# A four-layer graph network on one core: how the edge lists, their neighbours and the first weights are fetched

## The chip, the cores and the metric

The kernel runs on 1 core of one Trainium2 chip. The metric is the device time of one execution in microseconds (us). Before the change it is 2734.12 us, the median of 3 runs (2732.61 to 2734.6).

## The reference, cut to what matters

There are 3125 nodes with 256 features (`x`) and 53125 edges, sorted by destination. Four layers follow one another; each normalises `x`, computes something per edge, reduces it per destination node and adds it to `x`.

```python
src, dst = src[argsort(dst)], dst[argsort(dst)]       # edges sorted by destination
h = maximum(layernorm(x), 0)
# layer 0: message passing with a sum
msg = relu(concat([h[src], h[dst]]) @ W_msg + b_msg)
agg = segment_sum(msg, dst)
u   = relu(concat([h, agg]) @ W_upd + b_upd)
x   = x + (u - mean(u)) * rsqrt(var(u) + 1e-5) * gamma + beta
# layer 1: sum, mean and max of edge attributes, and an MLP
# layer 2: attention over the edges (segment max, exp, segment sums)
# layer 3: maximum over weighted neighbours
g = relu(maximum(layernorm(x), 0) @ W_pool.T + b_pool)
neigh = segment_max(g[src] * edge_weight, dst)
x   = x + h @ W_self.T + b_self + neigh @ W_neigh.T + b_neigh
```

Because the edges are sorted by destination, a node's edges stand in a row. Whether an edge is the first or the last of its node is seen by comparing its destination with that of the edge before it and of the edge after it. This is why the kernel needs the neighbours of every edge, across the borders of its own tiling too.

## The kernel before, in words

The kernel is a row of stages, each a `nc.Block()` with one instruction stream per engine; a stage begins when all engines have ended the one before. The change touches three of them.

**The opening** (`opening`, from L252). It does three things at once.

- It loads `x` in five parts of five blocks of 125 nodes (SyncE's queue, L325), normalises it, and computes two tables: h times the upper half of W_msg (the source table) and h times the lower half plus bias (the window table). For each of the 25 blocks: ScalarE makes `h` (L376), TensorE turns it (L400), VectorE copies the turned block to `hT` (L476), TensorE multiplies (L411), ScalarE copies the source half out of PSUM (L381), VectorE adds the bias to the window half (L458), and SyncE (L333) and GpSimd (L357) store the two to HBM. `scales(c)` computes mean and scale of part c on VectorE; its one step on ScalarE is the square root (L373). `scales(0)` comes first; `scales(1)` stands in front of the `hT` copy of block 0, `scales(2)` in front of that of block 5, and so on.
- It reads the edge lists in rows of 128 edges, 104 rows x 4 on the partitions (`src_rows`, `dst_rows`), and makes from them the lines that mark first and last edges, with 17 dependent VectorE steps ("links", L491 to L513). Between one link and the next, VectorE does one block of the work above (`next_block`). The neighbour of each row's first edge is in a tile of its own, `before`, that of its last edge in `after`; each is filled by five DMAs. All these loads, and the two of `base` (first node of each row), are issued on ScalarE's queue (L365) ahead of everything else ScalarE does: 18 DMAs. VectorE waits for all 18 (`dve.wait_ge(loads, loaded)`) after `scales(0)` and before its first link.
- It does the same for the edges split in 128 lanes of 416 (`lane_dst`, `lane_last`, 3 more DMAs on ScalarE's queue, L368), with 16 further links (`lane_flags`, L545 to L564).

SyncE's order in the opening: the five loads of `x`, then a wait for the 17 links, then the three lines to HBM (L330), and only then the 25 stores of the source table, each behind a wait for its block. TensorE turns the edge rows after block 18 (`edges_at = lines_made + 1`).

**The message pass** (`sum_pass`, from L676) follows. GpSimd gathers 416 tiles of 128 rows of the source table by indirect DMA (L735), each with indices that SyncE fetches (L628). In this pass SyncE first loads the four weight tensors of the update stage (`self.load(sp, *ahead)`, L672), then the first indices.

**The last maximum** (`lane_max_pass`): a running maximum over each lane on VectorE. Three small VectorE memsets set its starting values to 0.

```python
transfers += [(before[:, q:q + 1], ends[q * RT - 2:(q + 1) * RT - 2, :]) for q in range(1, RQ - 1)]
...
act.wait_ge(clears, 4)
for tile, flat in transfers:
    act.dma_start(tile, flat, allow_slow_non_contiguous=True).then_inc(loads, 16)
```

Of the kernel before, what the change touches and what calls it, by code (L numbers as in the profile page):

```python
# [28 lines left out]
I32 = mybir.dt.int32  # L29
ALU = mybir.AluOpType  # L30
# [3 lines left out]
P = 1 << P_BITS  # L34
N = 3125
E = 53125
# [14 lines left out]
RQ = 4  # L51
RT = T // RQ
FULL = E // P
REST = E - FULL * P
# [10 lines left out]
FLT = 3.3895313892515355e38  # L65
# [5 lines left out]
LANE = -(-E // P)  # L71
LANES_FULL = E // LANE
# [36 lines left out]
class Kernel:  # L109
# [140 lines left out]
    def opening(self):  # L250
# [20 lines left out]
        lines_made, lane_steps = 17, 16  # L271
        edges_at = lines_made + 1
        with ExitStack() as ctx:
            def tmp(name, shape, dt=F32):
                return self.sb(name, shape, dt, ctx)
            raw = {k: tmp(k, [RT, RQ, P], I32) for k in ("src_rows", "dst_rows")}
            before, after = tmp("before", [RT, RQ], I32), tmp("after", [RT, RQ], I32)
            src_f, dst_f, other = (tmp(k, [RT, RQ, P]) for k in ("src_f", "dst_f", "other"))
            before_f, after_f = tmp("before_f", [RT, RQ]), tmp("after_f", [RT, RQ])
# [3 lines left out]
            lane_dst, lane_last = tmp("lane_dst", [P, LANE], I32), tmp("lane_last", [P, 1], I32)  # L283
            lane = {k: tmp(f"lane_{k}", [P, LANE]) for k in ("dst_f", "flag", "when")}
            lane.update({k: tmp(f"lane_{k}", [P, 1]) for k in ("last_f", "cut", "whole", "row", "own", "spare")})
# [11 lines left out]
            transfers = []  # L297
            for tile, flat in ((raw["dst_rows"], a["dst"]), (raw["src_rows"], a["src"])):
                transfers += [
                    (tile[:, 0:RQ - 1, :], flat[0:whole * P].rearrange("(q r c) -> r q c", r=RT, c=P)),  # L300
                    (tile[0:FULL - whole, RQ - 1, :], flat[whole * P:FULL * P].rearrange("(r c) -> r c", c=P)),
                    (tile[FULL - whole:FULL - whole + 1, RQ - 1, 0:REST],
                     flat[FULL * P:E].rearrange("(r c) -> r c", r=1))]
            dst = a["dst"]
            ends = dst[P:FULL * P].rearrange("(j c) -> j c", c=P)[:, P - 1:P]
            firsts = dst[P:FULL * P].rearrange("(j c) -> j c", c=P)[:, 0:1]
            transfers += [(before[1:2, 0:1], dst[P - 1:P].rearrange("(r c) -> r c", r=1)),
                          (before[2:RT, 0:1], ends[0:RT - 2, :])]
            transfers += [(before[:, q:q + 1], ends[q * RT - 2:(q + 1) * RT - 2, :]) for q in range(1, RQ - 1)]
            transfers += [(before[0:FULL + 1 - whole, RQ - 1:RQ], ends[whole - 2:FULL - 1, :])]  # L310
            transfers += [(after[:, q:q + 1], firsts[q * RT:(q + 1) * RT, :]) for q in range(RQ - 1)]
            transfers += [(after[0:FULL - 1 - whole, RQ - 1:RQ], firsts[whole:FULL - 1, :]),
                          (after[FULL - 1 - whole:FULL - whole, RQ - 1:RQ],
                           dst[FULL * P:FULL * P + 1].rearrange("(r c) -> r c", r=1))]
            transfers += [(self.base[0:1, 0:FULL], dst[0:FULL * P].rearrange("(j c) -> c j", c=P)[0:1, :]),
                          (self.base[0:1, FULL:FULL + 1], dst[FULL * P:FULL * P + 1].rearrange("(r c) -> r c", r=1))]
            lane_transfers = self.by_lanes(lane_dst, dst) + [
                (lane_last[1:P, :], dst[0:LANES_FULL * LANE].rearrange("(p t) -> p t", t=LANE)[:, LANE - 1:LANE])]
            loaded, lane_loaded = 16 * len(transfers), 16 * len(lane_transfers)

            with nc.Block() as block:
                @block.sync
                def _(sp):
                    for c, of in enumerate(parts):
                        sp.dma_start(self.x[:, of.start:of.stop, :], a["x"][of.start * NT:of.stop * NT, :].rearrange(  # L325
                            "(b p) d -> p b d", p=NT)).then_inc(x_in[c], 16)
                    sp.wait_ge(chain, lines_made)
                    lines = ((self.mask_line, mask), (self.place_line, rel16), (self.carry_line, carry))
                    for line, rows in lines:
                        sp.dma_start(line.rearrange("(q r c) -> r q c", r=RT, c=P), rows[:]).then_inc(lines_out, 16)  # L330
                    for b in range(NB):
                        sp.wait_ge(copied, b + 1)
                        sp.dma_start(self.source_table[b * NT:(b + 1) * NT, :], by_source[:, b, :]  # L333
                                     ).then_inc(sources_out, 16)
                    sp.wait_ge(lines_out, 16 * len(lines))
                    sp.wait_ge(sources_out, 16 * NB)

                @block.gpsimd
                def _(pool):
# [88 lines left out]
                def _(dve):  # L428
                    nc.vector.memset(lane_dst[:], N).then_inc(lane_clears, 1)
                    nc.vector.memset(lane_last[:], -1).then_inc(lane_clears, 1)  # L430
                    nc.vector.memset(raw["dst_rows"][:], -1).then_inc(clears, 1)
                    nc.vector.memset(raw["src_rows"][:], 0).then_inc(clears, 1)
                    nc.vector.memset(before[:], -1).then_inc(clears, 1)
                    nc.vector.memset(after[:], -1).then_inc(clears, 1)
# [56 lines left out]
                    link(nc.vector.tensor_copy(src_f[:], raw["src_rows"][:]))  # L491
                    link(nc.vector.tensor_copy(dst_f[:], raw["dst_rows"][:]))
                    link(nc.vector.tensor_copy(before_f[:], before[:]))
                    link(nc.vector.tensor_copy(after_f[:], after[:]))

                    link(nc.vector.tensor_tensor(rel[:], dst_f[:], dst_f[:, :, 0:1].to_broadcast([RT, RQ, P]),
                                                 ALU.subtract))
# [7 lines left out]

                    link(nc.vector.tensor_copy(other[:, :, 1:P], dst_f[:, :, 0:P - 1]))
                    link(nc.vector.tensor_copy(other[:, :, 0:1], before_f[:].unsqueeze(2)))
                    link(nc.vector.tensor_tensor(flag[:], dst_f[:], other[:], ALU.not_equal))
# [6 lines left out]
                    self.lane_flags(dve, lane, lane_loads, lane_loaded, lane_dst, lane_last, lane_marks, when_made,  # L515
# [13 lines left out]
    def lane_flags(self, dve, lane, loads, loaded, dst, last, marks, when_made, lane_steps, fill, placed):  # L529
# [16 lines left out]
        link(nc.vector.tensor_copy(lane["last_f"][:], last[:]))  # L546
        link(nc.vector.tensor_tensor(flag[:, 1:LANE], dst_f[:, 1:LANE], dst_f[:, 0:LANE - 1], ALU.not_equal))
        link(nc.vector.tensor_tensor(flag[:, 0:1], dst_f[:, 0:1], lane["last_f"][:], ALU.not_equal))
# [125 lines left out]
    def sum_pass(self, name, table, width, window_table, window_width, attention, ahead=None):  # L674
# [14 lines left out]
        with ExitStack() as ctx:  # L689
# [14 lines left out]
            with nc.Block() as block:  # L704
                @block.sync
                def _(sp):
# [15 lines left out]
                    if ahead:  # L722
                        self.load(sp, *ahead)
# [88 lines left out]
                def _(act):  # L812
                    if attention:
                        act.wait_ge(zeroed, 1)

# [1225 lines left out]
    def lane_max_pass(self, name, table, w_self, loaded, biases):  # L2041
# [13 lines left out]
        with ExitStack() as ctx:  # L2055
# [20 lines left out]
            with nc.Block() as block:  # L2076
# [99 lines left out]
                def _(dve):  # L2176
                    nc.vector.memset(none[:], 0.0).then_inc(cleared, 1)
                    nc.vector.memset(ends[:, :, 0:1], 0.0).then_inc(cleared, 1)
# [4 lines left out]
                    nc.vector.memset(end[:], 0.0).then_inc(stepped, 1)  # L2183
# [85 lines left out]
```

## Time and profile before

| | us |
|---|---|
| median of 3 runs | 2734.12 |
| profiled execution, its own time | 2734.72 |
| its span | 2732.6 |
| PE busy | 1354.9 |
| DVE busy | 1588.9 |
| POOL busy | 1390.0 |
| ACT busy | 672.6 |

PE is TensorE's matmuls, PEld its weight loads, DVE is VectorE, ACT ScalarE, POOL GpSimd, SP SyncE. A name with q (ACTq, SPq) is the engine's sequencer, where DMAs are issued; the duration of such a row is how long the issue held that queue, not the transfer. In brackets behind a row of the timeline stands how long the engine sat idle before it, and what ended the wait. No engine is busy for more than 58% of the span: the stages have different limits, so the profile has to be read stage by stage. The page's slices show DMA, TensorE and VectorE nearly idle at the very start of the span, and the opening ends at about 126 us.

### The profile page before, as it was taken

To read this page: it belongs to the slowest core of one execution; us is meant where nothing else is said; L and a number is where in the kernel's file an instruction comes from. 1 tells how busy PE (TensorE), PEld (TensorE's weight loads), DVE (VectorE), ACT (ScalarE), POOL (GpSimd) and SP (SyncE) were. 2 spreads that over 40 slices of the span, in tenths; PEclk is the share of its full clock that TensorE was granted. 3 is DMA by queue.
4 is the path that set the end of the run, shared out by engine and by line. 5 is a ranking of instruction groups with operands and counts; after the bars stand their busy time and mean duration, and the time that the engine had idled before them with its cause. 6 is when DMAs were issued, how large, how long until landed. Compare 5 with 4: busy or idle time off the path is not lost. (4 is left out here: it accounts for less than half of the span.)

```text
span 2732.6 us, 26946 instructions
## 1 busy us (share of the span) xinstructions
PE 1354.9 (50%) x7570; PEld 1070.0 (39%) x7570; DVE 1588.9 (58%) x3262; ACT 672.6 (25%) x1528; POOL 1390.0 (51%) x1444
## 2 busy tenths in 40 slices
PE   3577877877669999997993000000002411111104
PEld 2466766776569999554553000000001300000003
DVE  2467777776769999731213776677675334433432
ACT  1112222221547777111111000000002233333331
POOL 2177777776300000301104777777744377777774
PEclk9889999999879999998997555555555655555557
DMA  2477777875065564101002666666642466666664
GB/s 79 118 236 237 233 233 235 238 228 151 1 181 153 154 154 117 42 2 17 13 12 63 201 216 218 201 208 214 211 161 65 139 213 208 209 212 207 211 212 134
DMA packets 272030, 433.06 MB, mean 158 GB/s; under 512 B 108749, under 2 KB 181031, under 8 KB 271883
## 3 DMA queue, kind: packets, MB, share of 16 engines
q1 hardware_dynamic: 202635, 247.61, 27.3%
q0 software_dynamic: 66784, 183.09, 24.9%
q8 instruction: 62, 1.02, 0.2%
q10 hardware_dynamic: 2464, 0.64, 0.1%
q14 instruction: 85, 0.70, 0.1%
HBM read 302.15 MB, written 128.80 MB: 158 GB/s over the span
## 5 line engine op out<-in xcount | busy, mean ns | idle before, releaser
L1757 POOL DMA_INDIRECT att_rows<-att_table,lane_source x416 | 416.4, 1001 | 126.7 <-issue 126.7
L2083 POOL DMA_INDIRECT best_rows<-message_source_table,lane_source x416 | 393.3, 946 | 167.5 <-issue 126.4
L735 POOL DMA_INDIRECT msg_rows<-message_source_table,msg_index x416 | 400.0, 962 | 147.8 <-issue 125.2
L2194 DVE SCALAR_TENSOR_TENSOR best_state<-best_state,lane_line,best_ps_rows 128x256 f32<-128x256 f32 x416 | 199.8, 480 | 316.2 <-ACT best_ps_rows L2108 297.9
L863 PE MATMUL msg_ps_sum<-msg_by_edge,msg_rows 128*128 128x128 f32 x1664 | 232.4, 299 | 109.3 <-DVE aggT L795 107.6
L1789 PE MATMUL att_ps_upto<-ident,att_largest 128*4 128x128 f32 x1 | 0.4, 375 | 564.1 <-DVE att_largest L1854 564.1
L863 PEld LDWEIGHTS msg_ps_sum<-msg_by_edge,msg_rows 128*128 128x128 f32 x1664 | 218.0, 210 | 140.3 <-issue 139.1
L2108 ACT ACTIVATE best_ps_rows<-best_rows,lane_weight 128x256 f32<-128x256 f32 x416 | 173.5, 462 | 359.2 <-DMA best_rows<-message_source_table,lane_source 359.2
L2142 PE MATMUL best_ps_self<-w_selfT,hT 128*125 128x256 f32 x100 | 51.7, 671 | 398.3 <-DVE x L2200 387.2
L847 PE MATMUL msg_ps_window<-msg_window,msg_by_node 128*128 128x256 f32 x832 | 209.0, 397 | 26.5 <-DMA msg_window<-message_window_table 21.4
L1789 PEld LDWEIGHTS att_ps_upto<-ident,att_largest 128*4 128x4 f32 x1 | 0.1, 83 | 564.8 <-DVE att_largest L1854 564.8
L818 ACT ACTIVATE msg_rows<-msg_rows 128x1024 f32<-128x1024 f32 x104 | 109.9, 1057 | 443.8 <-DVE msg_rows L760 443.8
L1089 PE MATMUL attr_ps_placed<-attr_ends,attr_by_edge 128*97 128x128 f32 x1664 | 201.0, 274 | 0.3 <-ACT aggT L998 0.3
L760 DVE TENSOR_TENSOR msg_rows<-msg_ps_window,msg_rows 128x1024 f32<-128x1024 f32 x104 | 126.9, 1220 | 127.4 <-DMA msg_rows<-message_source_table,msg_index 125.9
L1876 DVE SCALAR_TENSOR_TENSOR aggT<-aggT,lane_carry,att_rows 128x260 f32<-128x260 f32 x388 | 190.3, 491 | 13.6
L2142 PEld LDWEIGHTS best_ps_self<-w_selfT,hT 128*125 128x125 f32 x100 | 28.9, 320 | 420.7 <-DVE x L2200 403.8
L1089 PEld LDWEIGHTS attr_ps_placed<-attr_ends,attr_by_edge 128*97 128x97 f32 x1664 | 186.2, 165 | 0.5 <-issue 0.5
L795 DVE TENSOR_TENSOR aggT<-aggT,msg_ps_sum 128x256 f32 x416 | 172.0, 413 | 24.2 <-DVE aggT L795 20.7
L847 PEld LDWEIGHTS msg_ps_window<-msg_window,msg_by_node 128*128 128x128 f32 x832 | 160.3, 203 | 46.7 <-DVE msg_by_node L748 21.6
L1347 POOL MEMSET att_wc<- 128x512 f32 x1 | 0.5, 519 | 337.1 <-POOLq L907 337.1
L1366 POOL DMA_INDIRECT att_terms<-aggT,first_edge x25 | 29.5, 1178 | 275.5 <-ACT aggT L1533 195.1
L998 ACT COPY aggT<-attr_ps_placed 97x256 f32 x416 | 158.3, 380 | 42.1 <-ACT aggT L998 27.9
(290 smaller groups left out, 2711.9 us busy)
## 6 DMA issues: line engine op xcount, KB each, us to landing
att_states<-aggT SPq DMA_DIRECT2D x104, 528.0 KB
msg_window<-message_window_table SPq DMA_DIRECT2D x416, 128.0 KB
best_states<-best_state SPq DMA_DIRECT2D x104, 512.0 KB
attr_rows<-in_edge_attr SPq DMA_DIRECT2D x103, 192.0 KB, 3.3
msg_line<-place_line SPq DMA_DIRECT2D x52, 256.0 KB, 4.9
attr_line<-mask_line SPq DMA_DIRECT2D x52, 256.0 KB, 3.9
attr_carry<-carry_line SPq DMA_DIRECT2D x52, 256.0 KB
msg_rows<-message_source_table,msg_index POOLq DMA_INDIRECT x416
```

Of the source, the lines that this page charges most:

```text
L735: nc.gpsimd.indirect_dma_start(rows[:, s, t, :], None, table, bass.IndirectOffsetOnAxis(ap=index[:, s, t:t + 1], axis=0)).then_inc(self.ro ...
L760: nc.vector.tensor_tensor(rows[:, s, :, :], ps_window[s % 2][:], rows[:, s, :, :], ALU.add).then_inc(ev["added"], 1)
L795: nc.vector.tensor_tensor(at, at, ps_sum[s % 2][:, t, :, :], ALU.add).then_inc(tile_added[t], 1)
L847: last = nc.tensor.matmul(ps_window[s % 2][:, t, :], by_node[:, s % BUFS, t * P:(t + 1) * P], window[:, s % BUFS, t, k * window_width:(k + ...
L863: last = nc.tensor.matmul(ps_sum[s % 2][:, t, k, :], rows[:, s, t, k * P:(k + 1) * P], by_edge[:, s % BUFS, t, :], start=True, stop=True)
L998: nc.scalar.copy(outT[:, :, bass.ds(bases[t], P)], ps_placed[s % 2][:, t, :, :]).then_inc(stored[t], 1)
L1089: last = nc.tensor.matmul(ps_placed[s % 2][:, t, k, :], by_edge[:, s % BUFS, t, k * bw:(k + 1) * bw], ends[:, s % BUFS, t, :], start=True, ...
L1757: nc.gpsimd.indirect_dma_start(rows[:, t % ring, :], None, self.attention_table, bass.IndirectOffsetOnAxis(ap=self.lane_source[:, t:t + 1] ...
L1876: nc.vector.scalar_tensor_tensor(out=state[:, t % held, 0:H * HS], in0=carried[:] if starts else state[:, (t - 1) % held, 0:H * HS], scala ...
L2083: nc.gpsimd.indirect_dma_start(rows[:, g % SLOTS, t, :], None, table, bass.IndirectOffsetOnAxis(ap=self.lane_source[:, g * TG + t:g * TG + ...
L2108: last = nc.scalar.activation(weighed_row(n), rows[:, g % SLOTS, t, :], ACT.Copy, scale=self.lane_weight[:, n:n + 1])
L2194: nc.vector.scalar_tensor_tensor(out=state[:, g % STATE_BUFS, t, :], in0=before, scalar=self.lane_line[:, n:n + 1], in1=weighed_row(n), op ...
```

## The change

- The tiles of destinations get two more columns: a row is fetched together with its left and right neighbour, as one run of 130 numbers that overlaps the next row's run. `before` and `after` and their ten DMAs go, and so do six links. The lanes get one more column in the same way; `lane_last` and two links go. In all there are 11 and 14 links.
- The eight edge-row loads are issued on GpSimd's queue, ahead of the loads of W_msg and its bias. ScalarE's queue keeps only the three lane loads, now split in rows 0, 1 to 126, and 127.
- The two `base` loads go to SyncE's queue, behind `x`.
- SyncE stores the source table's first 12 blocks, then waits for the links and stores the three lines, then goes on with the blocks. TensorE turns the edge rows after block 12.
- GpSimd's clearing of `aggT` is three memsets instead of one.
- In the message pass the update weights are loaded from ScalarE's queue instead of SyncE's.
- In the last maximum the starting values are the lowest number, not 0.

```diff
-        lines_made, lane_steps = 17, 16
+        lines_made, lane_steps = 11, 14
...
+            def run_of(first, rows, size):
+                return bass.AP(dst.tensor, dst.offset + first, [[step, n] for step, n in rows] + [[1, size]])
+            full_rows = FULL - whole
+            transfers = [
+                (dst_rows[0:1, 0, 1:P + 2], run_of(0, [(P, 1)], P + 1)),
+                (dst_rows[1:RT, 0, :], run_of(P - 1, [(P, RT - 1)], P + 2)),
+                (dst_rows[:, 1:RQ - 1, :], run_of(RT * P - 1, [(P, RT), (RT * P, RQ - 2)], P + 2)),
+                (dst_rows[0:full_rows, RQ - 1, :], run_of(whole * P - 1, [(P, full_rows)], P + 2)),
+                (dst_rows[full_rows:full_rows + 1, RQ - 1, 0:REST + 1], run_of(FULL * P - 1, [(P, 1)], REST + 1)),
+                (src_rows[:, 0:RQ - 1, :], src[0:whole * P].rearrange("(q r c) -> r q c", r=RT, c=P)),
+                (src_rows[0:full_rows, RQ - 1, :], src[whole * P:FULL * P].rearrange("(r c) -> r c", c=P)),
+                (src_rows[full_rows:full_rows + 1, RQ - 1, 0:REST], src[FULL * P:E].rearrange("(r c) -> r c", r=1))]
+            lane_transfers = [
+                (lane_dst[0:1, 1:LANE + 1], run_of(0, [(LANE, 1)], LANE)),
+                (lane_dst[1:LANES_FULL, :], run_of(LANE - 1, [(LANE, LANES_FULL - 1)], LANE + 1)),
+                (lane_dst[LANES_FULL:P, 0:LANE_REST + 1],
+                 run_of(LANES_FULL * LANE - 1, [(LANE, 1)], LANE_REST + 1))]
...
 SyncE, opening
-                    sp.wait_ge(chain, lines_made)
+                    for tile, flat in first_nodes:
+                        sp.dma_start(tile, flat, allow_slow_non_contiguous=True).then_inc(lines_out, 16)
-                    for line, rows in lines:
-                        sp.dma_start(line.rearrange("(q r c) -> r q c", r=RT, c=P), rows[:]).then_inc(lines_out, 16)
                     for b in range(NB):
+                        if b == edges_at:
+                            sp.wait_ge(chain, lines_made)
+                            for line, rows in lines:
+                                sp.dma_start(line.rearrange("(q r c) -> r q c", r=RT, c=P), rows[:]
+                                             ).then_inc(lines_out, 16)
                         sp.wait_ge(copied, b + 1)
...
 GpSimd, opening
+                    pool.wait_ge(clears, 2)
+                    for tile, flat in transfers:
+                        pool.dma_start(tile, flat, allow_slow_non_contiguous=True).then_inc(loads, 16)
...
-                    nc.gpsimd.memset(self.aggT[:], 0.0)
+                    for k in range(3):
+                        nc.gpsimd.memset(self.aggT[:, k, :], 0.0)
...
 ScalarE, opening
-                    act.wait_ge(clears, 4)
-                    for tile, flat in transfers:
-                        act.dma_start(tile, flat, allow_slow_non_contiguous=True).then_inc(loads, 16)
...
 VectorE, opening (the neighbours are slices of the same tile)
+                    own = dst_f[:, :, 1:P + 1]
-                    link(nc.vector.tensor_copy(other[:, :, 0:P - 1], dst_f[:, :, 1:P]))
-                    link(nc.vector.tensor_copy(other[:, :, P - 1:P], after_f[:].unsqueeze(2)))
-                    link(nc.vector.tensor_tensor(flag[:], dst_f[:], other[:], ALU.not_equal))
+                    link(nc.vector.tensor_tensor(flag[:], own, dst_f[:, :, 2:P + 2], ALU.not_equal))
...
 message pass
-                    if ahead:
-                        self.load(sp, *ahead)
...
+                    if ahead:
+                        self.load(act, *ahead)
...
 last maximum
-                    nc.vector.memset(ends[:, :, 0:1], 0.0).then_inc(cleared, 1)
+                    nc.vector.memset(ends[:, :, 0:1], -FLT).then_inc(cleared, 1)
...
-                    nc.vector.memset(end[:], 0.0).then_inc(stepped, 1)
+                    nc.vector.memset(end[:], -FLT).then_inc(stepped, 1)
```

## Rows read from the trace of the kernel before

**Rows 1.** One of the page's costliest groups: busy, mean ns | idle before, releaser.

```profile
L735 POOL DMA_INDIRECT msg_rows<-message_source_table,msg_index x416 | 400.0, 962 | 147.8 <-issue 125.2
```

**Rows 2.** GpSimd's waits, whole run: us in total, times, longest.

```profile
POOL msg_rows L735 <- issue: 125.2, 411, 0.3
...
POOL msg_rows L735 <- DMA msg_index<-source: 21.4, 1, 21.4
...
POOL msg_rows L735 <- PE msg_ps_sum L863: 1.2, 4, 0.3
```

**Rows 3.** Timeline of the first 50 us: start, duration, instruction, [idle <- releaser].

```profile
0.76 27.83 SPq L325 DMA_DIRECT2D x<-in_x  x5
...
1.57 1.69 POOL L347 DMA_DIRECT2D msg_w<-in_L_gnn_W_msg  x2
...
2.49 8.64 ACTq L365 DMA_DIRECT2D dst_rows<-in_dst  x3
...
3.23 0.60 POOL L350 DMA_DIRECT2D msg_bias<-in_L_gnn_b_msg  x1
...
4.04 8.28 POOL L352 MEMSET aggT<- 128x9759 f32 x1
11.15 9.07 ACTq L365 DMA_DIRECT2D src_rows<-in_src  x3
...
12.25 1.73 DVE L572 BATCH_NORM_STATS2 stats<-x 125x6 f32<-125x256 f32 x5 [9.39 <-DMA x<-in_x]
...
26.26 4.61 ACTq L365 DMA_DIRECT2D base<-in_dst  x2
30.91 9.79 ACTq L368 DMA_DIRECT2D lane_dst<-in_dst  x2
...
41.03 1.28 ACT L373 ACT_TABLE_LOAD   x1 [41.03 <-issue]
...
42.56 0.19 DVE L449 RECIPROCAL norm_rs<-norm_sd 125x5 f32<-125x5 f32 x1 [28.04 <-ACT norm_sd L373]
...
43.21 1.72 DVE L572 BATCH_NORM_STATS2 stats<-x 125x6 f32<-125x256 f32 x5
...
46.05 0.41 DVE L476 COPY hT<-norm_ps 128x250 f32<-128x250 f32 x1
```

**Rows 4.** Stretches of the opening: busy of each engine, clock, DMA share, GB/s.

```profile
20.00:25.00 5.00, 0.00 (x0) 0.00 (x0) 0.00 (x0) 0.00 (x0) 0.00 (x0) 1.00 0.38 118
...
36.00:39.00 3.00, 0.00 (x0) 0.00 (x0) 0.00 (x0) 0.00 (x0) 0.00 (x0) 1.00 0.07 24
```

**Rows 5.** DMA issues of 0 to 45 us: KB each, median us to landing.

```profile
x<-in_x SPq DMA_DIRECT2D x5, 625.0 KB
...
msg_bias<-in_L_gnn_b_msg POOLq DMA_DIRECT2D x1, 125.0 KB, 8.1
```

**Rows 6.** DMA issues of 40 to 110 us, the same columns.

```profile
message_window_table<-msg_out POOLq DMA_DIRECT2D x23, 125.0 KB, 2.2
```

**Rows 7.** Timeline from 80 us to the message pass.

```profile
90.44 29.09 SPq L333 DMA_DIRECT2D message_source_table<-h  x25
...
110.87 0.37 ACT L381 COPY h<-msg_table_ps_s 125x256 f32<-125x256 f32 x1 [1.57 <-PE msg_table_ps_w L411]
...
112.60 0.37 ACT L381 COPY h<-msg_table_ps_s 125x256 f32<-125x256 f32 x1 [1.35 <-PE msg_table_ps_w L411]
...
113.32 0.53 POOL L357 DMA_DIRECT2D message_window_table<-msg_out  x1 [1.20 <-DVE msg_out L458]
...
...
126.12 0.43 SPq L672 DMA_DIRECT2D upd_w<-in_L_gnn_W_upd  x1
...
127.86 1.21 SPq L628 DMA_DIRECT2D msg_index<-source  x2
...
135.23 1.10 POOL L735 DMA_INDIRECT msg_rows<-message_source_table,msg_index  x1 [21.38 <-DMA msg_index<-source]
```

**Rows 8.** One of VectorE's links, timeline at 57 us.

```profile
57.46 0.41 DVE L499 COPY other<-dst_f 104x508 f32<-104x508 f32 x1
```

More of the change, by code:

```diff
@@ L275, in tmp @@
                 return self.sb(name, shape, dt, ctx)
[L276 to L279, printed above, removed]
+            src_rows, dst_rows = tmp("src_rows", [RT, RQ, P], I32), tmp("dst_rows", [RT, RQ, P + 2], I32)
+            src_f, dst_f, other = tmp("src_f", [RT, RQ, P]), tmp("dst_f", [RT, RQ, P + 2]), tmp("other", [RT, RQ, P])
             rel, rel_end, flag = (tmp(k, [RT, RQ, P]) for k in ("rel", "rel_end", "flag"))
@@ L282, in opening @@
             carry = tmp("carry", [RT, RQ, P], BF16)
-            lane_dst, lane_last = tmp("lane_dst", [P, LANE], I32), tmp("lane_last", [P, 1], I32)
-            lane = {k: tmp(f"lane_{k}", [P, LANE]) for k in ("dst_f", "flag", "when")}
-            lane.update({k: tmp(f"lane_{k}", [P, 1]) for k in ("last_f", "cut", "whole", "row", "own", "spare")})
+            lane_dst = tmp("lane_dst", [P, 1 + LANE], I32)
+            lane = {"dst_f": tmp("lane_dst_f", [P, 1 + LANE])}
+            lane.update({k: tmp(f"lane_{k}", [P, LANE]) for k in ("flag", "when")})
+            lane.update({k: tmp(f"lane_{k}", [P, 1]) for k in ("cut", "whole", "row", "own", "spare")})
             lane["spread"] = tmp("lane_spread", [P, P])
@@ L295, in opening @@
             ps_window = [self.ps(f"msg_table_ps_w{k}", [NT, D], ctx) for k in range(2)]
[L297 to L316, printed above, removed]
@@ L317, in opening @@
-            lane_transfers = self.by_lanes(lane_dst, dst) + [
-                (lane_last[1:P, :], dst[0:LANES_FULL * LANE].rearrange("(p t) -> p t", t=LANE)[:, LANE - 1:LANE])]
+            src, dst = a["src"], a["dst"]
+            def run_of(first, rows, size):
[10 more added lines that the diff above has]
+                (src_rows[full_rows:full_rows + 1, RQ - 1, 0:REST], src[FULL * P:E].rearrange("(r c) -> r c", r=1))]
@@ new lines, in opening @@
+            lane_transfers = [
[3 more added lines that the diff above has]
+                 run_of(LANES_FULL * LANE - 1, [(LANE, 1)], LANE_REST + 1))]
+            first_nodes = [
+                (self.base[0:1, 0:FULL], dst[0:FULL * P].rearrange("(j c) -> c j", c=P)[0:1, :]),
+                (self.base[0:1, FULL:FULL + 1], dst[FULL * P:FULL * P + 1].rearrange("(r c) -> r c", r=1))]
@@ L334, in _ @@
                                      ).then_inc(sources_out, 16)
-                    sp.wait_ge(lines_out, 16 * len(lines))
+                    sp.wait_ge(lines_out, 16 * (len(first_nodes) + len(lines)))
                     sp.wait_ge(sources_out, 16 * NB)
@@ L428, in _ @@
                 def _(dve):
+                    nc.vector.memset(dst_rows[:], -1).then_inc(clears, 1)
+                    nc.vector.memset(src_rows[:], 0).then_inc(clears, 1)
                     nc.vector.memset(lane_dst[:], N).then_inc(lane_clears, 1)
[L430 to L434, printed above, removed]
+                    dve.wait_ge(lane_clears, 1)
+                    nc.vector.memset(lane_dst[0:1, 0:1], -1).then_inc(lane_clears, 1)
                     nc.vector.memset(self.ones[:], 1.0)
@@ L490, in _ @@
                     dve.wait_ge(loads, loaded)
[L491 to L497, printed above, removed]
-                    link(nc.vector.tensor_copy(other[:, :, 0:P - 1], dst_f[:, :, 1:P]))
-                    link(nc.vector.tensor_copy(other[:, :, P - 1:P], after_f[:].unsqueeze(2)))
-                    link(nc.vector.tensor_tensor(flag[:], dst_f[:], other[:], ALU.not_equal))
+                    link(nc.vector.tensor_copy(dst_f[:], dst_rows[:]))
+                    link(nc.vector.tensor_copy(src_f[:], src_rows[:]))
+                    own = dst_f[:, :, 1:P + 1]
+                    link(nc.vector.tensor_tensor(rel[:], own, dst_f[:, :, 1:2].to_broadcast([RT, RQ, P]), ALU.subtract))
+                    link(nc.vector.tensor_tensor(flag[:], own, dst_f[:, :, 2:P + 2], ALU.not_equal))
                     link(nc.vector.scalar_tensor_tensor(out=rel_end[:], in0=rel[:], scalar=1.0, in1=flag[:],
@@ L504, in _ @@
                     link(nc.vector.tensor_scalar(rel_end[:], rel_end[:], -1.0, None, ALU.add))
-                    link(nc.vector.tensor_copy(other[:, :, 1:P], dst_f[:, :, 0:P - 1]))
-                    link(nc.vector.tensor_copy(other[:, :, 0:1], before_f[:].unsqueeze(2)))
-                    link(nc.vector.tensor_tensor(flag[:], dst_f[:], other[:], ALU.not_equal))
+                    link(nc.vector.tensor_tensor(flag[:], own, dst_f[:, :, 0:P], ALU.not_equal))
                     link(nc.vector.tensor_scalar(other[:], flag[:], -FLT, FLT, ALU.mult, ALU.add))
@@ L514, in _ @@
                     assert steps == lines_made and block_at < edges_at
-                    self.lane_flags(dve, lane, lane_loads, lane_loaded, lane_dst, lane_last, lane_marks, when_made,
+                    self.lane_flags(dve, lane, lane_loads, lane_loaded, lane_dst, lane_marks, when_made,
                                     lane_steps, next_block, edges_placed)
@@ L527, in by_lanes, with lane_flags @@
                  flat[LANES_FULL * LANE:E].rearrange("(r c) -> r c", r=1))]
-    def lane_flags(self, dve, lane, loads, loaded, dst, last, marks, when_made, lane_steps, fill, placed):
+    def lane_flags(self, dve, lane, loads, loaded, dst, marks, when_made, lane_steps, fill, placed):
         nc = self.nc
@@ L545, in lane_flags @@
         link(nc.vector.tensor_copy(dst_f[:], dst[:]))
-        link(nc.vector.tensor_copy(lane["last_f"][:], last[:]))
-        link(nc.vector.tensor_tensor(flag[:, 1:LANE], dst_f[:, 1:LANE], dst_f[:, 0:LANE - 1], ALU.not_equal))
-        link(nc.vector.tensor_tensor(flag[:, 0:1], dst_f[:, 0:1], lane["last_f"][:], ALU.not_equal))
+        link(nc.vector.tensor_tensor(flag[:], dst_f[:, 1:LANE + 1], dst_f[:, 0:LANE], ALU.not_equal))
         link(nc.vector.tensor_scalar(self.lane_line[:], flag[:], -FLT, FLT, ALU.mult, ALU.add))
```

## The prediction, written before the changed kernel was run

> **What bounds the kernel now.** I read the page's groups first. GpSimd issues 416 gathers in the message pass, 962 ns each [rows 1]. Its waits say what paces the message pass: 125.2 us are gaps of 0.3 us between gathers that nothing else explains, 21.4 us are one wait at the very start, for the first indices, and only 1.2 us are waits for anything downstream [rows 2]. So from its first gather, at 135.23 us [rows 7], the pass runs at GpSimd's own pace for 400.0 + 125.2 us [rows 1, 2]. Whatever moves that first gather moves the end of the pass by as much. The stages behind it start one after the other and contain nothing that the change touches but three memsets, so the same shift should reach the end of the run.
>
> That makes the opening the place to look. In its timeline the reader is to see a hole: `x`'s first part has landed at 12.25 us (VectorE's statistics start there), but VectorE then sits for 28.04 us until ScalarE delivers one square root [rows 3]. ScalarE was not computing. Its queue was issuing DMAs back to back from 2.49 us to about 41 us; the ends of that row of issues are dst_rows, 8.64 us, src_rows, 9.07 us, base, 4.61 us, and lane_dst, 9.79 us [rows 3]. The first `hT` copy, which opens the 25 blocks, comes at 46.05 us. From there the blocks run at a pace that TensorE sets (ScalarE waits for the matmuls before each copy), and the last copy begins at 112.60 us [rows 3, 7]. A second hole is at the other end. SyncE begins to store the source table only at 90.44 us, behind its wait for the 17 links, and needs 29.09 us for the 25 stores, to 119.53 us. By then the last copy is 6.6 us old, and the next stage's first SyncE row is at 126.12 us [rows 7].
>
> **First part: the start of the blocks.** ScalarE loses 18 of its 21 DMA issues. What it keeps starts when VectorE's memsets are done, at about 2.5 us. If the three lane issues took as long as the old two did, 9.79 us, ScalarE would be free at 12.3 us, and with the table load that follows (1.28 us) at 13.6 us. The square root of part 0 cannot be asked for before its statistics end, at 12.25 + 1.73 = 14.0 us, in any case [rows 3]. So ScalarE's queue is off the path, whether the lane issues cost 10 us or 1.
>
> The next to be late is VectorE's input. Two things are needed: the eight edge-row loads, and part 1 of `x`, since `scales(1)` stands in front of block 0's `hT` copy. `x` moves at 118 GB/s [rows 4], and a part is 625 KB [rows 5], so a part takes 640,000 B / 118 GB/s = 5.4 us. I put part 0 at 12.2 us as before (ScalarE's traffic beside it goes, GpSimd's comes), with bounds: 8 us if nothing shares with it (issue at 0.76, 5.4 us, and 1.8 us until it lands, my estimate), 14 us if the moved rows hurt it more. Part 1 is then at 17.6 us, and the `hT` copy is 46.05 - 43.21 = 2.84 us behind the start of its statistics [rows 3]: 20.4 us. In the kernel before it was 46.05. **Gain 25.6 us**, bounds 23.6 to 29.6.
>
> Are GpSimd's loads there in time? No row shows these odd runs on GpSimd's queue. Near rows: its issue of 125 runs of 1 KB takes 0.53 to 0.60 us, two of 256 runs take 1.69 us [rows 3, 7]; that is 0.3 us plus 2.1 ns a run. The eight issues have 1, 103, 208, 103, 1, 312, 103 and 1 runs, 832 in all: 8 x 0.3 + 832 x 0.0021 = 4.2 us. From 2.0 us they end at 6.2 us, W_msg and bias then at 8.5 us instead of 3.8. Landing takes 2.2 us in quiet and 8.1 us beside `x` [rows 6, 5], so the rows are there by 8 to 14 us, and the weights, which TensorE needs for block 0, by 11 to 17 us; they are wanted at about 15.5 and 17 us. The upper bound for the eight issues is what the same rows cost on ScalarE's queue, 8.64 + 9.07 = 17.7 us: then rows land at 22 to 28 us and the weights at up to 30 us, and 10 us of the gain go. The lower bound is that they are free. I take the 4.2 us, from the nearer rows. GpSimd's clearing of `aggT`, 8.28 us in one piece or three, then ends near 18 us, in front of its first store at about 25 us: nothing.
>
> A rule of the Trainium skill speaks against this move ("SBUF — State Buffer", the "DVE blocks DMA" trap): while VectorE is in a two-port mode, GpSimd can't write its DMA descriptors. In rows, VectorE does little before its wait of 9.39 us, which ends at 12.25 us, so it starts at 2.86 us [rows 3]. By the rule the issues, which begin at 2.0 us, would be delayed by 1 us at most, and the sum would stay; it gives the second rival below a part of its chance.
>
> The Trainium skill ("DMA: Bandwidth & Descriptors", why a DMA increments its semaphore by 16) also says that a DMA uses the largest number of engines up to 16 that divides its slowest dimension: 127 lanes get 1 engine, the new 126 get 14. The trace agrees for the old one: when lane_dst alone is left, DMA runs at 0.07 of 16 engines and 24 GB/s [rows 4]. By the rule the lane issue drops from 9.8 us to about 1 us; without it, it does not, and by the sentence above on ScalarE's queue neither moves the sum.
>
> **Second part: the blocks.** From the first `hT` copy to the last ScalarE copy it is 112.60 - 46.05 = 66.5 us [rows 3, 7]. Eight links go from VectorE, at most 0.41 us each [rows 8] (a row of 4 numbers less), so under 3.3 us in all. They lie beside TensorE: ScalarE waits 1.57 us for it before each copy of 0.37 us [rows 7], a block per 1.94 us, while VectorE has two operations of 0.41 us and a link in a block. What stays on the path is the `scales` at blocks 5, 10, 15 and the one turn of the edge rows, now behind block 12, not 18: as many as before. I count 0, with bounds of -3 and +3 us (stores to HBM now run beside all blocks). The last copy begins at 20.4 + 66.5 = 86.9 us.
>
> **Third part: the end of the opening.** SyncE leaves the `x` issues at 28 us, then issues `base` (4.61 us on the other queue) and starts storing at about 33 us, with some five blocks waiting. A store takes 29.09 / 25 = 1.16 us; a block takes 66.5 / 25 = 2.7 us. The five are made good within 5 x 1.16 / (1 - 1.16 / 2.7) = 10 us, and SyncE follows ScalarE from then on. The three line stores, short issues between two blocks, disappear in it. So the last store starts when the last copy ends, at 87.3 us, lasts 1.2 us and lands some 2.2 us later: 90.7 us. GpSimd's last store (0.7 us after the copy began, 0.53, 2.2) is done by 90.4. With 0.7 us for the change of stage I put SyncE's first row of the next stage at 91.4 us, against 126.12: **34.7 us** in all, so 9.1 us from this part. Bounds: 0 (the stores are late again, or it is the change of stage that costs what lies between 119.5 and 126.1) and 10.
>
> **Fourth part: the first gather.** From 126.12 to 135.23 us are 9.1 us: 1.74 us for four weight issues and 7.4 us from the index issue to the gather [rows 7], since the indices stand behind 512 KB of weights and three 125 KB rows in the same queue. With these on ScalarE's queue the index is SyncE's first issue. Alone it would land like a quiet DMA, 2.2 us [rows 6]; sharing the engines with the weights adds something; I take 3 us, bounds 2.2 and 7.4. ScalarE's first operation of the pass needs gathered rows and comes after that gather, so its four issues, 1.74 us, cost nothing. First gather at 91.4 + 3.0 = 94.4 us, against 135.23. **Gain 40.8 us** in all.
>
> **The last pass** has memsets of the same size with another number: 0.
>
> **Sum.** Against the profiled execution's own time, 2734.72 us (span 2732.6 and 2.1 around it), the forecast is 2734.72 - 40.8 = 2693.9 us. The median of the runs is 0.6 us lower, so 2693.3 us; I say 2694.
>
> **The rivals.**
> 1. *GpSimd's queue is slow with the rows.* The eight issues cost up to 17.7 us, or wait on `x`'s traffic; VectorE's wait for the loads or TensorE's for W_msg takes the place of ScalarE's. For it: bias landed 8.1 us after its issue [rows 5]. Against it: 2.1 ns a run. Up to 10 us are lost: 2697 to 2704, say 2701 us.
> 2. *The tail does not shrink.* The source stores are late again, because SyncE's queue holds `x` and `base` before them, or the indices still need 7 us. 9 us or 4 us are lost: 2698 to 2703 us.
> 3. *The gain is given back.* Some later stage waits for something that does not move, and the shift ends there. Nothing in the waits of GpSimd speaks for it, since the message pass has no slack. 2734 us.
> 4. *Slower: the runs of 130 fall apart into single numbers.* The runs overlap and start off their boundary; the rows of destinations then are 54,000 transfers of 4 bytes. The nearest row: `base`, 415 single numbers, 4.61 us for the two issues, so 11 ns each; 54,000 of them are 600 us in front of block 0, less the 41 us: about 3290 us. It decides as soon as the loads are later than some 15 + 41 = 56 us, which is 3,700 single numbers. Against it: the innermost step is 1 and both sides are contiguous, as in src_rows, which went in pieces of whole rows.
>
> **How the numbers follow.** Forecast 0.66, rival 1 0.15, rival 2 0.13, rival 3 0.03, rival 4 0.03. The predicted time is that of the first, 2694 us. Its own bounds add to about -7 and +8 us (part 0 earlier by 4, blocks 3; or later by 2, blocks 3, index 3). Low 2686 us; the high end takes in most of the first two rivals: 2705 us. A measurement of this kernel tells 0.2%, some 5.5 us, from no change. Faster 0.94, same 0.03, slower 0.03.
>
> **What would show it.** Right: ScalarE's first square root near 15 us, the first `hT` copy near 20 us, VectorE's only long wait before it that for `x`; SyncE's last source store beginning within 1 us of the last copy; first gather near 94 us, and the message pass still 548 us minus its start wait. Wrong: a VectorE wait for dst_rows or src_rows, a TensorE wait for msg_w behind 20 us, SyncE's stores still running 3 us after the last copy, or a last gather of the pass that moved by less than the first.

## The result and the profile after

The changed kernel takes 2698.6 us (median of 4 runs, 2696.31 to 2702.74), the kernel before 2733.36 us beside it: a ratio of 0.9875, 95% interval 0.9858 to 0.9892, 34.8 us less. The forecast was 2694, range 2686 to 2705. The profiled run is the slowest of the four (2702.74 us, span 2700.9).

Timeline of the changed kernel's first 23 us, which answers to [rows 3] (start, duration, engine or queue, line, operation, tiles; in brackets the idle time before and what ended it):

```profile
0.76 23.82 SPq L325 DMA_DIRECT2D x<-in_x  x5
2.28 3.17 POOL L352 DMA_DIRECT2D dst_rows<-in_dst  x5 [0.66 <-DVE src_rows L435]
2.56 1.23 ACTq L373 DMA_DIRECT2D lane_dst<-in_dst  x3
5.45 1.92 POOL L352 DMA_DIRECT2D src_rows<-in_src  x3
9.65 8.32 POOL L360 MEMSET aggT<- 128x3253 f32 x3
12.42 1.73 DVE L565 BATCH_NORM_STATS2 stats<-x 125x6 f32<-125x256 f32 x5 [9.66 <-DMA x<-in_x]
14.53 3.47 DVE L451 TENSOR_SCALAR norm_sd<-norm_mv 125x5 f32<-125x5 f32 x1
18.04 0.21 ACT L378 ACTIVATE norm_sd<-norm_sd 125x5 f32<-125x5 f32 x1 [12.94 <-DVE norm_sd L451]
19.34 1.73 DVE L565 BATCH_NORM_STATS2 stats<-x 125x6 f32<-125x256 f32 x5 [0.33 <-DMA x<-in_x]
22.19 0.41 DVE L480 COPY hT<-norm_ps 128x250 f32<-128x250 f32 x1
```

The first `hT` copy moved from 46.05 to 22.19 us. The square root waits for VectorE now: a `tensor_scalar` of five columns takes 3.47 us, and ends as GpSimd's memset does (9.65 + 8.32 = 17.97). The end of the opening in the same timeline, answering to [rows 7]:

```profile
76.77 11.70 SPq L337 DMA_DIRECT2D message_source_table<-h  x7
87.82 0.37 ACT L386 COPY h<-msg_table_ps_s 125x256 f32<-125x256 f32 x1 [1.35 <-PE msg_table_ps_w L416]
95.57 0.41 ACTq L665 DMA_DIRECT2D upd_w<-in_L_gnn_W_upd  x1
95.58 1.19 SPq L621 DMA_DIRECT2D msg_index<-source  x2
100.48 1.04 POOL L726 DMA_INDIRECT msg_rows<-message_source_table,msg_index  x1 [11.41 <-DMA msg_index<-source]
```

SyncE's last store ends 0.3 us after the last copy, yet the next stage begins 7.1 us later. The first gather moved by 34.75 us, from 135.23 to 100.48, and the median of the runs by 34.8. In the profiled pair the end of the run moved less: its span went from 2732.6 to 2700.9 us, 31.7 us. So the near equality of the first two numbers is in part chance.

### The profile page after: what moved, and what is told of

Same layout as the page of the kernel before. It is cut to its first block and busy times, and to the rows that moved or that the text cites. A ratio compares the mean times of both kernels' runs of the same rounds, so it can differ in the third digit from the quotient of the medians.

```text
span 2700.9 us, 26930 instructions
## 1 busy us (share of the span) xinstructions
PE 1357.2 (50%) x7570; PEld 1072.5 (40%) x7570; DVE 1590.9 (59%) x3252; ACT 673.0 (25%) x1528; POOL 1396.6 (52%) x1454
## 5 line engine op out<-in xcount | busy, mean ns | idle before, releaser
L786 DVE TENSOR_TENSOR aggT<-aggT,msg_ps_sum 128x256 f32 x416 | 172.7, 415 | 24.1 <-DVE aggT L786 20.4
```

The lines of the kernel that those rows point to most:

```text
L786: nc.vector.tensor_tensor(at, at, ps_sum[s % 2][:, t, :, :], ALU.add).then_inc(tile_added[t], 1)
```

## The experiments

The four times of the opening are starts in the profiled run, in us; "next stage" is the first row that any queue has in the message pass. The ratio is to the kernel before, run beside each.

| run | first `hT` copy | last ScalarE copy | next stage | first gather | median us | ratio, 95% |
|---|---|---|---|---|---|---|
| changed | 22.19 | 87.82 | 95.57 | 100.48 | 2698.6 | 0.9875, 0.9858-0.9892 |
| changed_again | 21.77 | 87.18 | 94.95 | 100.05 | 2699.73 | 0.987, 0.9854-0.9885 |
| u_act_queue | 37.80 | 102.28 | 109.44 | 116.72 | 2718.34 | 0.9947, 0.9929-0.9964 |
| u_sp_loads | 22.22 | 86.84 | 94.02 | 102.92 | 2703.92 | 0.9886, 0.987-0.9903 |
| u_sp_order | 21.94 | 83.50 | 91.08 | 96.17 | 2699.24 | 0.988, 0.9863-0.9897 |
| a_spread | 22.27 | 84.01 | 91.36 | 96.36 | 2701.42 | 0.9884, 0.9867-0.99 |
| x_16 | 21.77 | 87.32 | 95.67 | 100.65 | 2704.34 | 0.9895, 0.9878-0.9913 |
| x_16_spread | 17.77 | 79.10 | 86.69 | 91.92 | 2697.24 | 0.9876, 0.9858-0.9895 |
| d_tail | 22.04 | 87.58 | 94.04 | 99.15 | 2702.33 | 0.989, 0.9873-0.9907 |
| w_late | 22.16 | 87.64 | 95.43 | 98.25 | 2698.41 | 0.9875, 0.9858-0.9892 |
| tail_split | 22.02 | 87.55 | 90.85 | 95.86 | 2697.86 | 0.9867, 0.9852-0.9882 |
| lane_113 | 29.00 | 94.29 | 101.78 | 109.07 | 2707.61 | 0.9908, 0.989-0.9926 |
| best | 17.72 | 79.38 | 82.98 | 85.52 | 2690.18 | 0.9846, 0.9832-0.9859 |

**The queue of the edge rows** (u_act_queue: the loop over `transfers` back in ScalarE's stream).

> The changed kernel, but its eight edge-row loads are issued on ScalarE's queue again, ahead of the lane loads. Theory (the opening was held by how many DMAs stood in front of ScalarE and how they were shaped, 38.5 us of issues, of which before/after, base and the lanes were 20): ScalarE keeps about 18 us of issues plus 1.2 for the lanes, its first square root comes near 22 us instead of 18.0, the first hT copy near 26 us instead of 22.2, first gather near 104.5 us, total near 2703 us. Rival (it is GpSimd's queue that makes the gain): ScalarE is held to 35 us or more, the total is back to 2712 us or more.

The total is the rival's, with 20 us lost; its condition is not quite met, since ScalarE was free at 27.2 us and not at 35. The theory's 2703 us is refuted. The changed kernel's eight issues took 5.1 us on GpSimd; here they take 24.1 us, in this kernel's timeline:

```profile
2.00 15.79 ACTq L370 DMA_DIRECT2D dst_rows<-in_dst  x5
17.82 8.33 ACTq L370 DMA_DIRECT2D src_rows<-in_src  x3
28.53 0.21 ACT L378 ACTIVATE norm_sd<-norm_sd 125x5 f32<-125x5 f32 x1
34.60 0.43 DVE L495 CAST dst_f<-dst_rows 104x520 f32<-104x520 int32 x1 [5.44 <-DMA src_rows<-in_src]
```

Two things hold the blocks: the square root comes only at 28.53 us, and the rows, issued by 26.2 us, land at 34.6. The first `hT` copy came at 46.05 us in the kernel before, at 37.80 here and at 22.19 in the changed kernel: of the 23.9 us gained there, the queue of these eight loads is worth 15.6 and everything else in the change, fewer and wider loads included, 8.3.

**The queue of the update weights** (u_sp_loads: `self.load(sp, *ahead)` again).

> The changed kernel, but the four weight loads of the update stage are issued on SyncE's queue in front of the first indices again. Theory (the indices stood behind the weights in one queue): SyncE's first row of the pass stays at 95.6 us, from there to the first gather it is again 9.1 us instead of 4.9, so first gather at 104.7 us and total near 2703 us. Rival (the engines are shared by all queues, so the order of issue gives nothing but the 1.7 us of issuing): first gather at 102.2 us, total near 2700 us.

From SyncE's first row (94.02) to the first gather (102.92) it is 8.9 us against 4.9: 4.0 us, as the theory has it. A block phase 1.0 us shorter and an end of the stage 0.6 us shorter hide part of that in the gather's time. The total is near the theory's 2703 us too, but its interval overlaps that of the changed kernel.

**The same weights, later** (w_late).

```diff
+                        act.wait_ge(*self.landed(self.index_in, 0, 0, groups=PAIR))
                         self.load(act, *ahead)
```

> The changed kernel, but ScalarE waits for the first indices to land before it issues the four weight loads. Theory (the index transfer shares engines with the weights even from another queue): from SyncE's index issue to the first gather 2.5 to 3 us instead of 4.9, total near 2696.5 us. Rival (4.9 us is what an index transfer takes): no change, 2699 us.

Its timeline at the stage change:

```profile
95.43 1.35 SPq L621 DMA_DIRECT2D msg_index<-source  x2
...
98.25 1.04 POOL L726 DMA_INDIRECT msg_rows<-message_source_table,msg_index  x1 [9.37 <-DMA msg_index<-source]
```

2.8 us instead of 4.9: shown in the trace, too small for the medians. So the index transfer does share something with the weights, even from another queue.

**SyncE's order** (u_sp_order: wait for the links and the three lines ahead of all source stores).

> The changed kernel, but SyncE waits for the links and stores the three lines before its first source-table store, as before. Theory A (the order of SyncE's stores gave the 7 us at the end of the opening): SyncE's last store ends 7 us later than 88.5 us, next stage at 102.5 us, total near 2705 us. Theory B (with 11 links instead of 17, the links end near block 11 and the 13 blocks left are enough to catch up at 1.3 us a store; the shorter chain alone would have done it): last store ends at 88.5 to 90.5 us, next stage within 2 us of 95.6, total near 2699 us.

Its timeline, SyncE's queue in the block phase:

```profile
44.33 0.32 SPq L332 DMA_DIRECT2D mask_line<-mask  x1
...
45.79 38.36 SPq L335 DMA_DIRECT2D message_source_table<-h  x25
```

Theory B: SyncE has caught up, at 84.15 us, 0.3 us behind the last copy (all of it some 4 us earlier than forecast, by a shorter block phase). In the kernel before its wait ended at 89 us, with 24 us of blocks left for 29 us of stores; here it ends at 44 us, with 40 us left. That is enough; the new order gave nothing. Whether the links end earlier because they are fewer or because they start earlier was not separated.

**The memset** (a_spread: 20 memsets of 488 columns behind the stores).

> The changed kernel, but GpSimd clears aggT in 20 pieces, one behind each of its first 20 stores, instead of at 9.65 to 17.97 us. Theory (VectorE's 3.47 us tensor_scalar at 14.53 us was held until GpSimd's memset ended at 17.97; part 1 of x, landed at 19.3 us, was due right behind it): the tensor_scalar takes 0.17 us, ScalarE's first square root comes at 14.8 us, but the first hT copy stays within 0.5 us of 22.2 us, because x part 1 is still at 19.3; total unchanged near 2699 us. Rival (the memset set the start): first hT copy near 19 us, total near 2695 us.

Its timeline, VectorE in the start:

```profile
14.44 0.17 DVE L453 TENSOR_SCALAR norm_sd<-norm_mv 125x5 f32<-125x5 f32 x1
...
19.41 1.73 DVE L567 BATCH_NORM_STATS2 stats<-x 125x6 f32<-125x256 f32 x5 [3.80 <-DMA x<-in_x]
```

As the theory says: the `tensor_scalar` is free, and VectorE waits 3.80 us for part 1 of `x` instead.

**The load of x** (x_16; x_16_spread adds the spread memset).

```diff
+ for lo, hi in ((0, 112), (112, NT)):
+     sp.dma_start(self.x[lo:hi, of.start:of.stop, :], part[lo:hi, :, :]).then_inc(x_in[c], 16)
```

> The changed kernel, but each part of x is loaded by two DMAs, 112 and 13 of its 125 partitions, instead of one. Theory (one DMA with 125 partitions uses 5 of the 16 DMA engines and so sets the start; with that gone GpSimd's memset of aggT, 9.65 to 17.97 us, sets it by holding VectorE's second tensor_scalar): x part 0 landed at 6 us or earlier, part 1 by 9 us, first hT copy at about 18.7 us, 3.5 us earlier than in the changed kernel, total near 2695 us. Rival (x is bounded by the memory or shared with the edge rows, not by the engine count): parts 0 and 1 still near 12 and 19 us, first hT copy at 22 us, total 2699 us.

> The same split of x, and aggT cleared in 20 pieces behind GpSimd's stores. Theory: neither x nor the memset holds VectorE; what is last then is the landing of the edge rows or of W_msg, at 11 to 13 us; first hT copy at 12 to 14 us, total near 2690 us. Rival (the block phase is set by something later, so an early start is lost again): first hT copy at 13 us but last ScalarE copy less than 5 us earlier than in the changed kernel's runs (83.5 to 87.8 us), total 2696 us or more.

The timeline of x_16, then that of x_16_spread, VectorE in the start:

```profile
5.94 1.73 DVE L566 BATCH_NORM_STATS2 stats<-x 125x6 f32<-125x256 f32 x5 [3.19 <-DMA x<-in_x]
...
8.05 9.95 DVE L452 TENSOR_SCALAR norm_sd<-norm_mv 125x5 f32<-125x5 f32 x1
```

```profile
8.04 0.17 DVE L454 TENSOR_SCALAR norm_sd<-norm_mv 125x5 f32<-125x5 f32 x1
...
14.44 0.43 DVE L498 CAST dst_f<-dst_rows 104x520 f32<-104x520 int32 x1 [5.57 <-DMA src_rows<-in_src]
```

Part 0 lands 6.5 us earlier with the split, so the number of DMA engines did bound `x`. Alone it gains nothing, since the memset holds the first `tensor_scalar` (I had expected the second) until 18.0 us. With both gone the edge rows are last, at 14.4 us; the first `hT` copy, expected at 12 to 14 us, comes at 17.77, and the total is the rival's, though not for its reason (the last copy is 8.7 us earlier). The first gather is 8.6 us earlier than in the changed kernel, but only 4.4 of these come from the earlier start; 4.3 come from a block phase that ran at a higher clock (below).

The ratio shows none of it: 0.9876 against 0.9875. Later stages differ by several us from one profiled run to the next. The largest such difference lies between the message pass's last gather and the first gather of the search behind it (`search_slices`): 467.0 us in the changed kernel, 469.0 in x_16_spread, 473.5 in x_16, 465.3 to 473.5 over all. That covers the 6.0 us by which x_16's profiled run was longer than the changed kernel's; why it varies stays open.

**The tail** (d_tail: the window stores of blocks 21 to 24 on ScalarE's queue; tail_split: these and the source stores besides in 112 and 13 partitions).

> The changed kernel, but the window-table stores of the last four blocks are issued on ScalarE's queue instead of GpSimd's. Theory (after its last store has landed GpSimd spends some 3 us in emptying its own DMA queue before it lets the stage end, which was hidden in the kernel before behind SyncE's late stores): from the end of the last ScalarE copy to SyncE's first row of the next stage 4 to 4.5 us instead of 7.2 to 7.4, total near 2695.5 us. Rival (the 7 us are the landing of the last stores, whoever issues them): still 7 us, total near 2699 us.

> The changed kernel; for the last four blocks the window-table stores are issued on ScalarE's queue, and these and the source-table stores in two DMAs of 112 and 13 partitions. Theory (a 3 us emptying of GpSimd's queue ends the stage in the changed kernel, and in the variant before this one its place was taken by two queues whose 125-partition stores share 5 of 16 DMA engines): SyncE's first row of the next stage 4 us or less after the last ScalarE copy has ended, instead of 7.4 and 5.9; first gather at 93 to 97 us, total near 2695 us. Rival (stores need 5 us to land whatever is done): still 6 us.

The timeline of d_tail, then that of tail_split, at the stage change:

```profile
87.58 0.37 ACT L387 COPY h<-msg_table_ps_s 125x256 f32<-125x256 f32 x1 [1.35 <-PE msg_table_ps_w L422]
...
94.04 0.42 ACTq L671 DMA_DIRECT2D upd_w<-in_L_gnn_W_upd  x1
```

```profile
87.55 0.37 ACT L388 COPY h<-msg_table_ps_s 125x256 f32<-125x256 f32 x1 [1.35 <-PE msg_table_ps_w L424]
...
90.85 0.42 ACTq L673 DMA_DIRECT2D upd_w<-in_L_gnn_W_upd  x1
```

From the end of the last copy to the next stage: 7.4 us in the changed kernel, 6.1 in d_tail, 2.9 in tail_split. The trace's own record of GpSimd's emptying of its queue (DRAIN), which the views leave out, lasts 3.09 us in the changed kernel, from 91.93 to 95.02 us, and begins when GpSimd's last store has landed. In d_tail it is over at 86.59 us and in tail_split at 87.01, before the last block is done, so in both it is off the path. In d_tail the theory's 4 to 4.5 us did not come: the last stores landed later, at 93.4 us on SyncE's queue and 93.6 on ScalarE's, where the changed kernel has 91.4 and, on GpSimd's, 91.8. The trace records five landings for each unsplit store on SyncE's or ScalarE's queue and sixteen for one on GpSimd's. With the stores split, all had landed by 90.4 us. So the 3 us are shown, and so is the price of the unsplit shape. That the two queues' stores share the same five engines fits this but is inferred. In the totals neither run stands out (ratios 0.989 and 0.9867, against 0.9875 and 0.987 of the changed kernel).

**The lanes** (lane_113: lanes 1 to 113 and 114 to 126).

> The changed kernel, but lanes 1 to 126 are loaded by two DMAs of 113 and 13 lanes on ScalarE's queue instead of one of 126. Theory (the number of partitions decides how many DMA engines work; a prime number gets one): ScalarE's queue is held for 8 us or more, from 2.55 us to 11 us or later, instead of 1.2 us, and since the square root is wanted at 14.5 us at the earliest and came at 18.0, the first hT copy stays at 22 us and the total near 2699 us. Rival (126 or 113 makes no difference): 1.5 us of issues.

Its timeline in the start:

```profile
2.56 11.40 ACTq L374 DMA_DIRECT2D lane_dst<-in_dst  x4
...
26.14 1.73 DVE L566 BATCH_NORM_STATS2 stats<-x 125x6 f32<-125x256 f32 x5 [7.13 <-DMA x<-in_x]
```

ScalarE is held as expected, to 13.96 us, and harmlessly. The total was wrong: part 1 of `x` lands 7 us later. The trace records five landings for that part: four by 18.3 us, no later than in the changed kernel, and the fifth at 26.12. One DMA engine carries the 113 lanes beside its share of `x`.

**The control and the sum of it** (changed_again; best has both splits, the spread memset, the moved stores and w_late's wait).

> The changed kernel itself, timed again beside the next ones. Every theory: 2696 to 2703 us, a ratio to the kernel before of 0.987 to 0.989, and a first gather between 96 and 101 us: part of its spread comes from the granted clock of TensorE in the block phase, which took 61 to 66 us in runs that were alike in all else.

> The changed kernel with x loaded in 112 and 13 partitions, aggT cleared in pieces behind GpSimd's stores, the last four blocks' stores split and GpSimd's taken over by ScalarE's queue, and the update weights behind the first indices. Theory: first hT copy at 17.8 us (behind the edge rows' landing at 14.4 us), stage change 3.5 us and index wait 2 us shorter, first gather at 86 to 90 us, total near 2689 us. Rival (what is gained before the first gather is lost in later stages that do not start at the shift): first gather below 90 us but total 2695 us or more.

The timeline of best:

```profile
17.72 0.42 DVE L491 COPY hT<-norm_ps 128x250 f32<-128x250 f32 x1 [0.15 <-PE norm_ps L416]
...
79.38 0.37 ACT L391 COPY h<-msg_table_ps_s 125x256 f32<-125x256 f32 x1 [1.35 <-PE msg_table_ps_w L427]
...
82.98 1.19 SPq L632 DMA_DIRECT2D msg_index<-source  x2
```

It beats the kernel before, and very likely the changed one: 2690.18 us against 2699.73 beside it. The intervals of the ratios just overlap (0.9832-0.9859 and 0.9854-0.9885), but its five runs (2687.12 to 2693.61 us) lie below all but one of the eight runs of the changed kernel (2692.07 to 2702.74). The first gather is 15.0 us earlier than in the changed kernel's first profile: 4.5 by the start, 4.2 by the end of the stage, 2.4 by the indices, and 4.0 by the clock of the block phase, which the edits were not meant to touch.

## Why the prediction was right, and where its terms were off

The mechanism held, step by step; the range held the time. The terms, forecast and measured: first `hT` copy 20.4, 22.19 (+1.8); from there to the last copy 66.5, 65.6 (-0.9); to the next stage 4.5, 7.75 (+3.3); to the first gather 3.0, 4.9 (+1.9). Together +6.1 us, the 94.4 that became 100.48.

- *Start.* Part 0 was right (12.2, 12.42). The term that was too small is "a part takes 5.4 us": part 1 came 6.9 us later. The row it was taken from is a stretch without GpSimd's traffic; by the trace's landings parts 2 and 3, with GpSimd's loads over, followed after 5.6 and 5.3 us. GpSimd's issues were 5.1 us, not 4.2, and VectorE never waited for them. "GpSimd's clearing of `aggT`: nothing" was right only by luck: it held VectorE for 3.5 us in the shadow of `x`, and sets the start once `x` is faster. The Trainium skill's rule on that trap ("SBUF — State Buffer", SBUF: two separate sides) was weighed for descriptors alone. The other direction of the same lock, a VectorE operation that waits for a GpSimd one, is what the trace has (3.47 us, and 0.17 in a_spread). The prediction also ties the rule to its second rival, the tail; it bears on the first, GpSimd's queue.
- *Lanes.* "By the rule ... neither moves the sum" was wrong for a lane load that stays on one engine. The Trainium skill's rule ("DMA: Bandwidth & Descriptors", why a DMA increments its semaphore by 16) agrees with the trace (the issues with 126 lanes held ScalarE's queue for 1.23 us, those with 113 for 11.40), and I followed it to ScalarE's queue, not to the engine that `x` shares: 7 us in lane_113.
- *Blocks.* No change was forecast, and with 0.9 us none stands out from the spread. That spread goes with the granted clock. Two stretches of the windows view, of the changed kernel, then of u_sp_order (length, then busy time of PE, PEld, DVE, ACT and POOL with their instructions, the clock, the DMA share and GB/s):

```profile
35.00:45.00 10.00, 8.36 (x34) 6.95 (x35) 5.44 (x21) 3.89 (x9) 1.64 (x4) 0.83 0.44 131
45.00:55.00 10.00, 8.13 (x34) 6.52 (x33) 6.38 (x24) 3.90 (x9) 2.08 (x4) 0.83 0.30 94
```

```profile
35.00:45.00 10.00, 9.32 (x47) 8.05 (x48) 6.83 (x20) 3.94 (x9) 2.65 (x5) 1.00 0.25 64
45.00:55.00 10.00, 7.81 (x47) 6.46 (x45) 5.85 (x21) 4.15 (x10) 1.59 (x3) 1.00 0.60 150
```

  The clock is the third number from the end. At 0.83 part of the stretch ran at 1.2 GHz, after TensorE had waited for `scales`; at 1.00 all of it at 2.4. The phase took 65.6 and 61.6 us. In u_sp_order TensorE waited just as long for `scales` at 47 us (1.86 us, as at 36 us in the changed kernel), and the clock stayed at 1.00; why is open. Over all thirteen profiles of the table the phase took 61.3 to 61.7 us in four (u_sp_order, a_spread, x_16_spread, best) and 64.5 to 65.6 in the rest. Three of these four have the spread memset, so with one profile a kernel it can't be excluded that the memset has a part in it.
- *Tail.* The forecast had the stores' landing, not GpSimd's 3 us behind it. In the kernel before, SyncE's late stores had covered them: GpSimd's emptying was over at 122.1 us there, SyncE's last store landed at 125.6. What I credited to SyncE's order is due to the links ending earlier.
- *Indices.* The weights on the other queue still delayed them, by 2.1 us (w_late).
- *Afterwards.* The shift passed through the message pass, with 526.6 us of gathers against 526.5. In the last maximum the 416 gathers take 519.9 us against 519.7, so its memsets cost nothing that shows. The profiled pair lost 3 us on the way to the end. The largest piece, 1.8 us, lies behind the last of these gathers: from there to the end of the span it is 61.9 us in the kernel before and 62.5 to 64.6 in all thirteen profiles with the change. No run tells why; the price is small, but "the same shift should reach the end" held only to within it. Rival 1 was not this kernel's case. Rival 2's size, 5 us, came about, with another cause in the tail; its range, 2698 to 2703 us, holds the measured time as well, so the number alone does not tell it from the forecast.

## What to carry to other kernels

When a stage's late stores or loads are cleared away, list what they had covered on every other queue: here a 3 us emptying of GpSimd's queue and an 8 us memset. Follow a badly shaped DMA to the engines it shares, not only to the queue that issues it; 112 + 13 partitions instead of 125 brought the first part of `x` 6.5 us sooner. And judge an edit of a few us by the stage times in the trace when the clock and the later stages move the total by as much from run to run, and take the clock's part out of the stage times before crediting the edit.

## What was not expected of the hardware

The timeline of x_16:

```profile
8.83 0.58 POOL L358 DMA_DIRECT2D msg_bias<-in_L_gnn_b_msg  x1
...
9.64 8.32 POOL L361 MEMSET aggT<- 128x3253 f32 x3
```

The `tensor_scalar` is recorded from 8.05 us, 1.6 us before the memset that it waits for, while GpSimd was issuing DMAs; in x_16_spread the same operation at the same time took 0.17 us. Between the three memsets VectorE never got its turn. Why the hold begins before the memset does stays open.
